# Starting every scan one phase earlier in a hand-written schedule of 29 phases

## The reference

```python
x = x + attention(layernorm(x), ...)        # 16 heads of 8; the values are scaled by the softmax's row sum
x = x + ffn(layernorm(x), gate_w, w1, w2)   # 8 experts, each token goes to its best 2
x = x + scan(layernorm(x), W_x, W_dt, ...)  # 16 states
x = x + ffn(layernorm(x), gate_w, w1, w2)
# scan: delta = softplus(...); dA_cumsum = exp(reverse cumulative sum of delta * A)
#   xs = cumsum(delta * u * B * dA_cumsum) / (dA_cumsum + 1e-12);  y = sum_n(xs * C) + u * D
```

## Time and profile before

| | |
|---|---|
| time, median of 3 runs | 1312.56 us (1308.08 to 1318.05) |
| the profiled execution: its time, its span | 1314.99 us, 1313.3 us |
| busy share of the span: PE, PEld, DVE, ACT, POOL | 82%, 61%, 65%, 55%, 41% |
| mean granted TensorE clock | 0.834 |
| weight loads of the runs | 191 of 512 KB, median 4.4 us to landing |

### The profile page before, as it was taken

The page is one execution under the profiler, slowest core; times in us unless marked ns, Lnnn a source line. Parts: engine busy times, 40 slices in busy tenths (PEclk is TensorE's granted clock), DMA queues, the critical chain, the costliest instruction groups (busy, mean ns, idle before and its releaser), DMA issues. The chain is left out here.

```text
span 1313.3 us, 19768 instructions
## 1 busy us (share of the span) xinstructions
PE 1082.6 (82%) x5797; PEld 806.6 (61%) x5797; DVE 852.7 (65%) x2958; ACT 723.2 (55%) x2042; POOL 539.1 (41%) x588
## 2 busy tenths in 40 slices
PE   3778789968998887889896669888899999789883
PEld 2545468845666643466663348666777788577773
DVE  3565756676887878688878865565565666557331
ACT  3777667777876765677765334444344454332220
POOL 3200230026254555735347767333362454734142
PEclk9555559965998966589887689999899999889896
DMA  8400036504342200044320045426454474456783
GB/s 258 126 0 1 10 115 207 156 19 125 97 146 81 62 14 12 29 152 137 113 71 14 21 152 158 150 88 191 138 181 157 150 215 154 137 171 187 233 275 104
DMA packets 109723, 157.89 MB, mean 120 GB/s; under 512 B 10064, under 2 KB 79696, under 8 KB 109488
## 3 DMA queue, kind: packets, MB, share of 16 engines
q1 hardware_dynamic: 96736, 136.34, 33.5%
q0 software_dynamic: 8528, 18.19, 4.5%
q10 hardware_dynamic: 4352, 2.10, 0.6%
HBM read 129.52 MB, written 31.26 MB: 122 GB/s over the span
## 5 line engine op out<-in xcount | busy, mean ns | idle before, releaser
L631 POOL TENSOR_TENSOR rings<-Rs_b,Abc 128x512 f32<-128x512 f32 x128 | 163.2, 1277 | 329.9 <-DVE Pw L1029 328.1
L773 ACT ACTIVATE sc_bank<-sc_bank,nmx_b 128x256 f32<-128x256 f32 x512 | 228.1, 448 | 62.4 <-DVE nmx_b L974 61.8
L845 ACT ACTIVATE hid<-h_bank 128x512 f32<-128x512 f32 x191 | 113.0, 598 | 268.0 <-PE h_bank L1465 268.0
L1379 PE MATMUL sc_bank<-Pw,upto 128*128 128x512 f32 x256 | 161.0, 714 | 84.6 <-DVE Pw L1029 84.2
L1465 PE MATMUL h_bank<-xT,wring 128*128 128x128 f32 x1528 | 211.3, 294 | 22.3 <-DVE xT L1157 12.1
L1465 PEld LDWEIGHTS h_bank<-xT,wring 128*128 128x128 f32 x1528 | 193.0, 204 | 37.5 <-DVE xT L1157 21.5
L974 DVE TENSOR_REDUCE nmx_b<-sc_bank 128x2 f32<-128x512 f32 x256 | 172.7, 683 | 58.8 <-PE sc_bank L1320 57.5
L1474 PE MATMUL h_bank<-wring,hid 128*128 128x128 f32 x1528 | 196.8, 283 | 9.1 <-ACT hid L845 8.9
L1474 PEld LDWEIGHTS h_bank<-wring,hid 128*128 128x128 f32 x1528 | 185.5, 197 | 12.5 <-ACT hid L845 10.8
L1166 DVE COPY eos<-h_bank 128x128 f32<-128x128 f32 x191 | 53.6, 288 | 201.0 <-PE h_bank L1474 192.9
L682 POOL DMA_INDIRECT xg<-xnb,pos x128 | 126.8, 990 | 100.1 <-DVE pos L1133 44.2
(11 more groups left out here) (173 smaller groups left out, 1514.6 us busy)
## 6 DMA issues: line engine op xcount, KB each, us to landing
wring<-wcat SPq DMA_DIRECT2D x191, 512.0 KB, 4.4
stage<-xg SPq DMA_DIRECT2D x41, 256.0 KB, 5.7
yg<-eos SPq DMA_DIRECT2D x41, 256.0 KB, 5.5
wcat<-in_w SPq DMA_DIRECT2D x16, 256.0 KB, 5.6
xg<-stage SPq DMA_DIRECT2D x2, 1536.0 KB, 12.9
X<-in_x SPq DMA_DIRECT2D x16, 128.0 KB, 4.8
xg<-xnb,pos POOLq DMA_INDIRECT x128, 2.3
gbuf<-yg,pos POOLq DMA_INDIRECT x128, 4.3
```

Of the source, the lines that this page charges most:

```text
L631: pool.tensor_tensor(exp_slot(k).rearrange("p (n d) -> p n d", d=D), Rs[:, c].unsqueeze(1).broadcast_to([P, 4, D]), Abc[:, s].rearrange("p ...
L773: last = act.activation(s[:, c * L:(c + 1) * L], s[:, c * L:(c + 1) * L], ACT.Exp, bias=nmx_b[:, b % 2, c, r:r + 1], accum_out=Z_b[:, b % ...
L845: act.activation(hid[:, b % 2], hb[b % 2][:], ACT.Relu).then_inc(*run_act.done(f"h{b}", r))
L1379: last = pe.matmul(sc[2 + k % 2][:], w[:], v, start=(m == 0), stop=(m == len(products) - 1))
```

## The change

Scans start at phase 8 + b, so everything from the first front on lies one phase nearer to the attentions; PHASES falls from 29 to 28. The runs of layer 1 keep their first phases (6, 10, 14, 18) but must be stored before the gathers in half phase 10 of phases 7, 11, 15 and 19, so they get 26 half phases (25 events). The groups of layer 2 hold 5, 5, 3, 2 and 1 sequences (27, 27, 19, 15 and 11 blocks in place of 31, 23, 19, 15 and 11; the sum stays 99). FINAL moves with them.

```diff
-    GROUPS = {1: (4, 4, 4, 4), 2: (6, 4, 3, 2, 1)}
+    GROUPS = {1: (4, 4, 4, 4), 2: (5, 5, 3, 2, 1)}
@@
-    SCAN_FIRST = 9
+    SCAN_FIRST = 8
@@
-        RUN_FIRST = {(1, 0): (6, 0, 34), (1, 1): (10, 0, 38), (1, 2): (14, 0, 38), (1, 3): (18, 0, 34), (2, 0): (20, 4, 42),
-                     (2, 1): (23, 0, 26), (2, 2): (25, 0, 22), (2, 3): (26, 7, 17), (2, 4): (27, 9, 13)}
+        RUN_FIRST = {(1, 0): (6, 0, 26), (1, 1): (10, 0, 26), (1, 2): (14, 0, 26), (1, 3): (18, 0, 26), (2, 0): (19, 11, 34),
+                     (2, 1): (21, 14, 34), (2, 2): (24, 0, 22), (2, 3): (25, 7, 17), (2, 4): (26, 9, 13)}
@@
-        FINAL = [(23, 4, (0, 1)), (24, 4, (2, 3)), (25, 0, (4, 5)), (25, 5, (6, 7)), (25, 10, (8, 9)), (27, 1, (10, 11)), (27, 8, (12,)),
-                 (27, 12, (13, 14)), (28, 6, (15,))]
-        PHASES = 29
+        FINAL = [(22, 4, (0, 1)), (22, 10, (2, 3)), (24, 2, (4, 5)), (24, 7, (6, 7)), (24, 12, (8, 9)), (26, 1, (10, 11)), (26, 8, (12,)),
+                 (26, 12, (13, 14)), (27, 6, (15,))]
+        PHASES = 28
```

## The result

The changed kernel is slower: in 20 runs of each on the same chip, 1333.9 us against 1315.1, a ratio of 1.0124 with a 95% interval of 1.0099 to 1.0149, which is +16 us (13 to 20); the ratio leaves out two runs of the changed kernel, the profiled one among them, because they lie over 1.5% above its fastest. On chip 0 the ratio is 1.0092 (1.0059 to 1.0125). The forecast was 1343 and slower by 30: the side and the range hold, the size is nearly twice too large.

A forecast was written before the change was run, and what follows sets the result against it. PE was taken to set the pace where runs are on, with low clocks in phases without events. Stages of -20.5, +95.5, -46.8 and +2 gave +30.2 on 1312.6: 1343 us, range 1303 to 1366, own range 1326 to 1360.

The forecast's parts named there:

- What bounds the kernel: PE sets the pace where runs are on, 1.72 us an event; phases without events get no shorter, their clock falls.
- Phases 6 and 7: First stage, old phases 6 to 8: 51.5 and 35.5 us, together 87.0 against 107.51, so -20.5 us.
- busy price: Cost of an event taken from the growth of PE's busy time between phases 22 and 23: 2.18 us.
- Phases 8 to 16: Second stage, old phases 9 to 16: 526.0 us against 430.51, so +95.5 us.
- Phases 17 to 23: Third stage, old phases 17 to 24: the same 83 events over six phases, 371.5 us against 418.30, so -46.8.
- costed at nothing: Memsets, smaller routing tables, four gathers right behind a run's last block, and weight loads: all taken as covered, 0 us.
- price of phase 23: Phase 18, with 16 events, was put at 55.6 us from old phase 23, which took 55.62.
- The end: Last stage, before 175.28 us: same phases one earlier, one tighter seam at 24.0, +2 us, between 0 and 6.
- Events are free everywhere: Rival, chance 0.12: each phase costs what its kind cost, so -19 us, 1294 us.
- share of LDWEIGHTS: Argument for the free-events rival: phase 15 with six more events would load weights 51.7 us and fit in 58.
- Packed phases: Rival, chance 0.20: dense phases shrink to PE's busy time, 10 and 14 at 64.2, 11 and 15 at 58; 1318 us.
- Seams: Rival, chance 0.10: four gathers and the start of (2, 0) stall 20 to 25 us in all; 1366 us.

The follow-up runs named there:

- squeeze alone: Kernel before, scans still from phase 9, with only the layer 1 runs cut to 26 half phases: ratio to before 1.0064.
- the filling: Changed kernel with four unread constant matmuls per half phase in 7.10 to 9.15, 11.10 to 13.15 and 15.10 to 17.15: ratio to before 0.9951.
- the seam mended: Changed kernel with the layer 1 scatters spread over 8 half phases instead of 16: ratio to before 1.0014.

## Why the prediction was right in its side and too large

**What bounds the kernel.** Right in the main. Events in dense phases are paid at 1.4 to 1.6 us (squeeze alone, for 1.72 forecast), and a phase without events is long for its clock where this was tested and gave way (filled phase 12, and the two stretches at 1.00 and 0.63). Phase 13, which the prediction took as its example, gained 4.3 us of the filling up to 13.9 and gave it back behind a wait for Pw.

**Phases 6 and 7.** 51.8 and 32.25 us against 51.5 and 35.5. In phase 7 the busy price, given there as the bound of 32.6, was the right one.

**Phases 8 to 16.** 521.4 against 526.0, with misses of both signs. Phases 8, 9, 12 and 13 came at 36.4, 52.9, 58.1 and 62.2 for 37.9, 56.0, 57.9 and 62.2. Phases 11 and 15 came at 59.0 and 58.8 for 63.2: their last five half phases took what was forecast, but the two more events in the first eleven half phases cost nothing instead of 3.4 (42.8 us in phase 15, where the old one took 43.68). The clock in them is 0.94 for the old 0.92, which is likely a part of it; no run tests it. Phase 14 came at 66.8 for 68.5. Phase 10 came at 72.5 for 68.5, above the upper bound of 70.8: it starts at half clock and its rows are late; with the scatter done earlier it is 64.0, at the lower bound. Phase 16 was put 6 us too low and phase 17 7 too high, and by luck the two errors cancel. That the sums of the late scans (from sequence 7 on) move one phase forward was not in the forecast and is the likely reason; it was not tested.

**Phases 17 to 23.** 372.8 against 371.5, and that hides the step that failed: phase 18 was put at 55.6 and took 65.9. The prediction looks for seams at the runs' ends, at 19.11 and at 24.0. The start of a run behind its own scatter has no term in the sum and is not named under what is costed at nothing; phase 18 got the price of phase 23, which has no such start. The trace of before gave no warning by itself, since PE stood at 18.0 for Pw (6.6 us) and not for rows. With the seam mended, phase 18 is 56.7. Phases 20 and 21 came 5.2 and 3.1 under their forecast.

**The end.** +6.0 against +2 in this profile, +4.7 between chips 0 and 10. Three profiles on chip 4 with the same instructions took 174.6 to 175.8 us, level with the old end (175.28), so the +6.0 is not shown to be the change's.

**The size.** The sum of +30.2 met the profile's +27.9, but not the +16 of 20 runs, and that it met the profile is luck: it was made from one execution and met another that was the longest of its kind, some 9 us above its median, and the misses of the phases, up to 10 us each, have both signs. On chip 0 the difference is smaller still (+12 us); old phase 9 alone, seen on chip 10, is 9.3 us longer there than on the first chip. The forecast's own range is also not what its bounds give: those of phases 9, 10, 11, 14 and 15 add up to 1318 to 1353 us, not 1326 to 1360. The measured 1329 (1312.56 times the ratio) lies in both.

**The rivals.** *Events are free everywhere* fell with the squeeze alone. The share of LDWEIGHTS, by which, with the share of peak FLOPs, the Trainium skill (Perfetto Trace Analysis, Identifying the Most-Contended Engine) judges headroom, promised room that was not there: phase 14 went from 37.53 of 59.87 us to 46.66 of 66.78, and its length grew all the same. *Packed phases* (1318) was half right: 11 and 15 did take 59, but 10 and 14 did not pack to 64 (72.5 and 66.8) until the scatter was moved (64.0 and 65.0). The measured time lies between this rival and the forecast's 1343. *Seams* was right in kind and wrong in place: the gathers cost nothing that shows, the runs' starts did. With the scatters done earlier, the kernel is about 1% faster and level with before, so the net effect of that one line is as large as the whole measured loss. By subtraction the squeeze (+9 us alone) and the dropped phase would then about cancel. That is not shown: the dropped phase was not run by itself, since the runs would not end before their gathers.

## What to carry to other kernels

When a hand-written schedule is shortened, look at every producer whose spread depends on what else the phase holds: a scatter that ended long before its reader may now end right at it. A wait that does not show in the old trace may only stand behind a longer one, so cost each start of a run by its own chain (last scatter, load of rows, load of weights) and not by the wait that was seen. Sums by phase tell where time goes, but the size of a change of 1% needs more than one profiled execution of each side, and both on one chip.

## What was not expected of the hardware

Doubling PE's matmuls in a phase made it shorter: 58.1 us with 125 records at clock 0.62, 48.8 us with 253 at 1.00. The same in phase 13 gained only 0.5 us (62.2 at 0.60, 61.7 at 0.86). Five half phases of the same kind took 10.6 us at 1.00 and 15.9 at 0.63. A wait of 6.7 us for rows was followed by a half phase at 0.50 that took 6.06 us, where it takes 2.33 at 1.00. And chips differed by 3% in the kernel before (1315 us on the first and 1352 on chips 0 and 10), while a phase without scatters took 52.79 on the first and 52.80 on chip 10.
